# A state-space layer and a gated feed-forward net in one kernel: ScalarE's long stretches cut into parts with slots of their own

## The chip, the cores and the metric

The kernel runs on one core of a Trainium2 chip, all in float32. The metric is the time on the device in microseconds (us), the median of several runs; lower is better. Two kernels are compared on one chip.

## The reference

Input x is 2 sequences of 1024 tokens with 512 channels. Cut to what matters:

```python
xn = x * rsqrt(mean(x * x) + 1e-6) * norm_w
xn = xn * sigmoid((xn @ select_proj_w.T + select_proj_b) * select_gate)
delta, B, C = split(xn @ x_proj_w.T, 128)                # 128 wide each
dt = softplus(delta @ dt_proj_w.T + dt_proj_b)           # 512 wide
h = exp(dt * A) * h + (dt * xn) * B                      # per token, h is 512 x 128
y = sum_n h * C
x = layernorm(x + (y + x * D_param) @ out_proj_w.T)
out = layernorm(x + (silu(x @ w_gate.T) * (x @ w_up.T)) @ w_down.T)   # hidden 2048
```

(The D_param term takes the layer's own input x.) Everything but the recurrence over the 1024 tokens is matrix products and elementwise work; the recurrence is serial.

## The kernel before, in words

**The recurrence.** The state sits as 128 partitions (n) by 2 x 512 columns. VectorE makes four instructions a step t: two products `m = a * h` (L686, one for each sequence, SBUF to PSUM) and two sums into the new `h` (L706 or L709). If another engine has multiplied the row `u_bc` by B beforehand, the sum is a plain add (L706); if not, it is a scalar_tensor_tensor (L709) that multiplies as well. GpSimd scales one row of four in most pairs of steps (`on_pool`, L593), ScalarE three more (`on_act`, L1000) in stretches called quiet and where the load that the table LOAD gives for the steps' stages is at most 5. The exponentials `a` come from TensorE products (L1200, called P below) and a ScalarE Exp of 128x2048 (L981, called E); P writes four PSUM banks with no second buffer, so P and E alternate. `a` is a ring of 4 blocks of 4 steps: E of a slot that is a multiple of 8 waits until VectorE has left the oldest block. TensorE also forms y (L1276, "y rows", two steps at a time, 8 matmuls), and `h` is a ring of 6: VectorE's sum of step t waits until y of step t-6 is formed. `u_bc` is a ring of 5, filled from DRAM (`u_scratch`) by SyncE's queue.

**The order.** A chunk is 128 steps of the recurrence and has 256 slots, two a step, about 1.26 us each. TensorE's, ScalarE's and GpSimd's programs are written in order of slot, each engine in order. E stands at slots 0, 4, 8, ..., P two slots earlier (2, 6, 10, ...), the y rows at 0, 4, 8, ..., each ahead of what the plan puts at the same slot. Around these, a planner (`timetable`) places the stages of two threads: one prepares the next chunk (`stages_before`: x_in, sq, ms, root, xn, sel, gate, mask, xs, xp, dtp, pre, soft, c1 to c4, ut, utc), one finishes the chunk before (`stages_behind`: xd, ya, yt, ymc, outp, ln1, vt, vtc, 16 x gu with act, 16 x down with dnc, back, ln2, and the weight loads, tile). A stage is a tuple (name, index, slots until the next one). Both threads write one PSUM bank, `work`: a stage that fills it may only be placed after the slot in which the last user is emptied, and a thread that comes too early is moved to that slot. The stages c1 to c4, gm and gp and a few more (PIECES) run on GpSimd, one group every 4 slots.

**The last chunk.** In chunk 7 the thread of x = 6 runs as ever, and from slot 132 a second one (x = LAST = 7) finishes the first half of chunk 7; the second half is finished behind the recurrence, on 5 banks. Weight tiles (512 KB each, L916, ScalarE's queue) of x = 7 turn in 3 places. The second half's tiles go into the ring `a` as it comes free: ScalarE issues 8 of them at the start of step 1017 (slot 242, ahead of what is planned there), 4 at step 1021 (slot 250) and the other places later. TensorE's last y rows stand behind everything that is planned in the chunk.

**Stages that matter here.** `layer_norm` (L855 to L871) is 6 activations, 2 reads of an accumulator and a table load, in one run on ScalarE. `soft` (softplus) is a table load and 6 activations; `sq` is a square of 128x1024 and four scalings of 128x256. The parts of the plan before that the change moves, as the planner's rule gives them for chunks 1 to 6 (a stroke marks the thread that finishes):

```
6 sq0 | 11 ymc0' | 12 ms | 16 root | 17 20 outp' | 24 ln10' | 25 yt1' | 28 ymc1' | 29 32 sel 36 gate0 |
37 40 sel 44 gate1 | 45 48 outp' | 52 ln11' | 54 vt0' | 59 vt1' | 63 68 73 xp | 78 dtp0 82 soft0 |
82 to 181 gu', act' | 136 dtp1 140 soft1 | 184 to 232 down' | 206 ut0 209 utc0 210 ut1 213 utc1 |
236 back0' 240 ln20' 242 back1' 246 ln21'
```

Chunk 7: 121 to 157 down' of x = 6 with yt0' of x = 7 at 148; 160 163 outp', 166 ln10', 167 back0', 170 ln20', 171 vt0', 175 back1', 178 ln21', 179 to 226 gu' and act', 227 to 245 down', 247 back0', 250 ln20'. The tiles of the last downs are loaded at 231, 234, 236 and 239 (tiles 20 to 23).

Of the kernel before, what the change touches and what calls it, by code (L numbers as in the profile page):

```python
# [6 lines left out]
P = 128  # L7
# [9 lines left out]
GP = P // G  # L17
# [19 lines left out]
LOAD = {"sq": 24, "root": 16, "gate": 8, "mask": 5, "xpc": 2, "pre": 6, "soft": 40, "utc": 4, "ymc": 4, "ln1": 36, "vtc": 4,  # L37
        "act": 10, "dnc": 2, "ln2": 36}
# [35 lines left out]
def stages_before():  # L74

    yield from [("x_in", 0, 6), ("sq", 0, 4), ("ms", 0, 4), ("root", 0, 4)]
    for j in range(2):
        yield "xn", j, 0
    for j in range(2):
        yield from [("sel", 2 * j, 3), ("sel", 2 * j + 1, 4), ("gate", j, 1)]  # L80
    yield "mask", 0, 1
    yield "mask", 1, 3
    for j in range(2):
        yield "xs", j, 0
    for m in range(3):
        yield from [("xp", m, 4), ("xpc", m, 1)]
    for j in range(2):
        yield from [("dtp", j, 3), ("pre", j, 1), ("soft", j, 7), ("c1", j, 0), ("c2", j, 0), ("c3", j, 0), ("c4", j, 0)]
    for b in range(BATCH):
        yield from [("ut", b, 3), ("utc", b, 1)]  # L90
# [12 lines left out]
def stages_behind(x):  # L103

    both, ws, wide = x < LAST, halves(x), int(x < LAST - 1)
    ahead = W_RING if both else (TILES_14 if x == LAST else HB)
    if x <= LAST:
        for j in range(ahead):
            yield "tile", j, 0
    for w in ws:  # L110
        yield from [("xd", w, 0), ("ya", w, 0)] if w == ws[0] else [("xd*", w, 0), ("ya*", w, 0)]
    for w in ws:
        yield from [("yt", w, 2 + wide), ("ymc", w, 2)]
        if x == UNITS - 1:
# [12 lines left out]
    yield "rest", 0, 2 * wide  # L127
    for m in range(KB):
        for q in range(4):
            yield "down", 4 * m + q, (2 + q % 2 * wide if both else 1)  # L130
            if q % 2 and HB + ahead + 2 * m + q // 2 < TILES:
                yield "tile", HB + ahead + 2 * m + q // 2, 0
        yield "dnc", m, 1
    for w in ws:
        yield from [("back", w, 3 + wide), ("ln2", w, 1 + wide)]


def timetable(c):
# [6 lines left out]
    if c < LAST:  # L145
        threads.append([0, c + 1, list(stages_before())])
    if c == LAST:
        threads.append([2 * SLOTS * GP + 4, LAST, list(stages_behind(LAST))])
    if c > 0:
        x = c - 1 if c < CHUNKS else LAST + 1  # L150
        threads.append([0, x, list(stages_behind(x))])
    emptied, taken = 0, {}
    while threads:
        thread = min(threads, key=lambda t: t[0])
        slot, x, stages = thread
# [3 lines left out]
        if first and slot < emptied:  # L159
            thread[0] = emptied  # L160
            continue
# [25 lines left out]
def build(nc, xT, x_rows, vecs, d_row, sel_wT, xproj_wT, dt_wT, out_wT, A_log, gu_w, down_w, out_rows):  # L187
# [5 lines left out]
    with ctx:  # L193
# [46 lines left out]
        stat = sb("stat", [P, 8])  # L240
# [67 lines left out]
        def window_of(x, w):  # L308
# [33 lines left out]
        s_xd, s_ya, s_yt, s_outp, s_ln, s_vt, s_gu, s_th, s_sg, s_gm, s_gated, s_down, s_back = (  # L342
            sem(s) for s in ("s_xd", "s_ya", "s_yt", "s_outp", "s_ln", "s_vt", "s_gu", "s_th", "s_sg", "s_gm",
# [374 lines left out]
        def scalar(e):  # L718
# [3 lines left out]
            def before(x, stage, j):  # L722
# [6 lines left out]
                elif stage == "sq":  # L729
# [4 lines left out]
                    e.activation(T[:, :, :], U[:, :, :], ACT.Square).then_inc(s_sq, 1)  # L734
                    e.wait_ge(s_sq, x + 1)
# [36 lines left out]
                elif stage == "soft":  # L772
                    n = 5 * (2 * (x - 1) + j)
                    log_table()
                    e.wait_ge(s_work, emptied("dtp", x, j))
                    e.wait_ge(s_c2, 2 * x + j)
                    if j == 0:
                        e.wait_ge(d_us, 16 * BATCH * x)
                    e.activation(t_exp, pre[:, :, :], ACT.Abs).then_inc(s_soft, 1)
                    e.wait_ge(s_soft, n + 1)  # L780
                    e.activation(pre[:, :, :], pre[:, :, :], ACT.Relu).then_inc(s_relu, 1)
                    e.activation(t_exp, t_exp, ACT.Exp, scale=-1.0).then_inc(s_soft, 1)
                    e.wait_ge(s_soft, n + 2)
                    if j == 0:
                        e.wait_ge(s_xs, 2 * (x + 1))
                    e.activation(T[:, both, :], t_exp, ACT.Ln, bias=one[:, :]).then_inc(s_soft, 1)
                    e.activation(t_one, t_exp, ACT.Identity, bias=one[:, :]).then_inc(s_soft, 1)
                    e.wait_ge(s_soft, n + 4)
                    e.activation(t_one, t_one, ACT.Identity, bias=minus_one[:, :]).then_inc(s_soft, 1)
# [104 lines left out]
            def behind(x, stage, j):  # L894
# [29 lines left out]
                elif stage == "ln1":  # L924
# [3 lines left out]
                    layer_norm(bank("outp", x, j), emptied("outp", x, j), x, j, norms[stage, x, j])  # L928
# [25 lines left out]
                elif stage == "ln2":  # L954
                    e.wait_ge(s_back, window_of(x, j) + 1)
                    layer_norm(bank("back", x, j), emptied("back", x, j), x, j, norms[stage, x, j])
                    e.wait_ge(s_ln, 6 * (norms[stage, x, j] + 1))
# [67 lines left out]
            for slot in sorted(plans[CHUNKS]):  # L1025
                for stage, x, j in plans[CHUNKS][slot]:
                    if stage in ("ln1", "ln2"):
                        root_behind(stage, x, j)
                    elif stage not in ("ymc", "vtc"):
# [3 lines left out]
        def tensor(e):  # L1033
# [52 lines left out]
            def behind(x, stage, j):  # L1086
# [42 lines left out]
                elif stage == "vt":  # L1129
                    dst = bank(stage, x, j) if x > LAST else take(stage, x, j)  # L1130
                    if x <= LAST:
                        e.wait_ge(s_ln, 6 * (norms["ln1", x, j] + 1))
# [214 lines left out]
```

## Time and profile before

| what | value |
|---|---|
| median of 3 runs | 2693.13 us (2690.42 to 2694.03) |
| profiled execution, its own time | 2687.74 us |
| its span in the profile | 2685.9 us |
| VectorE busy | 2584.4 us (96%) |
| TensorE busy | 2316.6 us (86%) |
| ScalarE busy | 1708.6 us (64%) |
| GpSimd busy | 1028.3 us (38%) |
| recurrence, first product to last sum | 38.4 to 2620.5 us |
| behind it | 65.4 us |

Busy is the union of an engine's instructions. Idle time ahead of an instruction is given with the event that ended it. On this core an idle engine costs nothing unless the one that ends the chain waits for it, so the table alone doesn't say what a faster engine is worth.

### The profile page before, as it was taken

To read this page: it belongs to the slowest core of one execution; us is meant where nothing else is said; L and a number is where in the kernel's file an instruction comes from. 1 tells how busy PE (TensorE), PEld (TensorE's weight loads), DVE (VectorE), ACT (ScalarE), POOL (GpSimd) and SP (SyncE) were. 2 spreads that over 40 slices of the span, in tenths; PEclk is the share of its full clock that TensorE was granted. 3 is DMA by queue.
4 is the path that set the end of the run, shared out by engine and by line. 5 is a ranking of instruction groups with operands and counts; after the bars stand their busy time and mean duration, and the time that the engine had idled before them with its cause. 6 is when DMAs were issued, how large, how long until landed. Compare 5 with 4: busy or idle time off the path is not lost.

```text
span 2685.9 us, 48350 instructions
## 1 busy us (share of the span) xinstructions
PE 2316.6 (86%) x17036; PEld 1290.5 (48%) x17036; DVE 2584.4 (96%) x4160; ACT 1708.6 (64%) x2229; POOL 1028.3 (38%) x1031
## 2 busy tenths in 40 slices
PE   7866678998789987899779997799977998899998
PEld 4322224554345543555345553455534554465567
DVE  6999999999999999999999999999999999999892
ACT  5687766667566665667656666566666667654643
POOL 2343333443434434344333443344333443344320
PEclk8999999999999989999889998899989999999899
DMA  4566665777667876678757786577866777788694
GB/s 171 197 213 227 228 236 211 281 277 270 237 223 277 284 266 223 238 275 292 254 195 247 279 290 243 201 267 277 278 241 209 279 279 271 239 289 308 228 357 151
DMA packets 192060, 672.16 MB, mean 250 GB/s; under 512 B 20944, under 2 KB 26064, under 8 KB 191824
## 3 DMA queue, kind: packets, MB, share of 16 engines
q1 hardware_dynamic: 152432, 544.02, 57.5%
q10 hardware_dynamic: 39392, 125.06, 13.3%
q8 instruction: 140, 2.29, 0.3%
q14 instruction: 96, 0.79, 0.1%
HBM read 660.61 MB, written 8.39 MB: 249 GB/s over the span
## 4 chain that ended last, share of the span: by engine, by line
PE 39%; DVE 28%; ACT 15%; issue 12%; DMA 6%; POOL 0%; ACTq 0%; DVEq 0%; POOLq 0%
DVE h L709 14%; PE banks L1200 11%; DVE banks L686 10%; PE banks L1036 10%; PE banks L1176 7%; PE banks L1276 7%; ACT a L981 6%; DVE h L706 4%; DMA u_bc<-u_scratch 4%; ACT L720 2%; DMA U<-in_xT 1%; PE banks L1128 1%; PE banks L1124 1%; ACT u_bc L1000 1%; ACT v L862 1%
## 5 line engine op out<-in xcount | busy, mean ns | idle before, releaser
L981 ACT ACTIVATE a<-banks 128x2048 f32<-128x2048 f32 x512 | 960.7, 1876 | 604.3 <-PE banks L1200 563.1
L686 DVE TENSOR_TENSOR banks<-a,h 128x512 f32<-128x512 f32 x2048 | 1324.1, 688 | 4.1 <-ACT a L981 4.1
L709 DVE SCALAR_TENSOR_TENSOR h<-u_bc,BCt,banks 128x512 f32<-128x512 f32 x1482 | 1038.2, 732 | 5.4 <-PE banks L1276 5.4
L581 POOL TENSOR_TENSOR dexp<-spread,dt 128x512 f32<-128x512 f32 x512 | 539.1, 1053 | 821.2 <-DVE banks L686 779.2
L1200 PE MATMUL banks<-dexp,A 32*128 32x256 f32 x8192 | 623.6, 421 | 150.6 <-ACT a L981 149.0
L1276 PE MATMUL banks<-h,cz 128*32 128x512 f32 x4096 | 667.9, 623 | 94.4 <-DVE h L706 64.7
L1200 PEld LDWEIGHTS banks<-dexp,A 32*128 32x128 f32 x8192 | 390.3, 195 | 484.4 <-ACT a L981 347.7
L1036 PE MATMUL banks<-vT,w_ring 128*128 128x256 f32 x1792 | 449.9, 394 | 7.6 <-ACT up L948 6.9
L1036 PEld LDWEIGHTS banks<-vT,w_ring 128*128 128x128 f32 x1792 | 323.8, 190 | 175.4 <-issue 118.2
L706 DVE TENSOR_TENSOR h<-u_bc,banks 128x512 f32<-128x512 f32 x566 | 367.5, 673 | 19.9 <-PE banks L1276 19.9
L593 POOL TENSOR_SCALAR u_bc<-u_bc,BCt 128x512 f32<-128x512 f32 x266 | 184.1, 692 | 404.6 <-DVE banks L686 394.3
L1276 PEld LDWEIGHTS banks<-h,cz 128*32 128x32 f32 x4096 | 102.4, 109 | 351.4 <-issue 342.1
L1000 ACT ACTIVATE u_bc<-u_bc,BCt 128x512 f32<-128x512 f32 x300 | 203.6, 713 | 66.8 <-DMA u_bc<-u_scratch 65.4
L1176 PE MATMUL banks<-gated,w_ring 128*128 128x256 f32 x896 | 224.3, 393 | 10.2 <-ACT vT L953 7.7
L1176 PEld LDWEIGHTS banks<-gated,w_ring 128*128 128x128 f32 x896 | 161.3, 190 | 95.0 <-issue 60.1
L946 ACT ACTIVATE sg<-banks 128x256 f32<-128x256 f32 (+1 forms) x144 | 51.9, 361 | 180.5 <-PE banks L1036 179.1
L1036 PE MATMUL banks<-U,w_sel 128*128 128x256 f32 x256 | 78.0, 460 | 42.0 <-ACT gated L923 20.8
L525 POOL TENSOR_TENSOR gated<-gated,up 128x512 f32<-128x512 f32 x56 | 71.5, 1278 | 82.5 <-DVE banks L686 81.0
L522 POOL TENSOR_TENSOR gated<-gated,sg 128x512 f32<-128x512 f32 x56 | 71.5, 1278 | 81.8 <-DVE banks L686 81.8
L1036 PEld LDWEIGHTS banks<-U,w_sel 128*128 128x128 f32 x256 | 55.2, 225 | 74.5 <-ACT dt L748 26.3
L720 ACT ACT_TABLE_LOAD x55 | 70.6, 1283 | 4.5 <-issue 2.3
L950 ACT ACTIVATE sg<-sg,half 128x256 f32<-128x256 f32 (+1 forms) x144 | 71.4, 496 | 0.0
(177 smaller groups left out, 1284.9 us busy)
## 6 DMA issues: line engine op xcount, KB each, us to landing
u_bc<-u_scratch SPq DMA_DIRECT2D x1021, 512.0 KB, 4.6
w_ring<-in_gu_w ACTq DMA_DIRECT2D x112, 512.0 KB, 5.5
w_ring<-in_down_w ACTq DMA_DIRECT2D x56, 512.0 KB, 5.7
a<-in_gu_w ACTq DMA_DIRECT2D x16, 512.0 KB, 12.7
a<-in_down_w ACTq DMA_DIRECT2D x8, 512.0 KB, 4.4
x_tok<-in_x_rows SPq DMA_DIRECT2D x15, 256.0 KB, 5.7
out_rows<-v ACTq DMA_DIRECT2D x15, 256.0 KB, 3.4
U<-in_xT ACTq DMA_DIRECT2D x7, 512.0 KB, 6.0
```

Source lines behind the costliest of these rows:

```text
L581: e.tensor_tensor(dexp[:, q % E_RING, :, :, :], spread[:, :].unsqueeze(1).unsqueeze(1).to_broadcast(shape), by_step[:, :, first:first + BS ...
L593: e.tensor_scalar(part, part, BCt[c % 2][:, 0, tl:tl + 1], 1.0, ALU.mult, ALU.mult).then_inc(s_zp, 1)
L686: e.tensor_tensor(m_ps[:, b, :], a[:, blk % A_RING, b, s, :], h[:, (t - 1) % H_RING, b * D:(b + 1) * D], ALU.mult).then_inc(s_m, 1)
L706: e.tensor_tensor(h[:, t % H_RING, part], u_bc[:, t % U_RING, part], m_ps[:, b, :], ALU.add).then_inc(s_h, 1)
L709: e.scalar_tensor_tensor(h[:, t % H_RING, part], u_bc[:, t % U_RING, part], BCt[c % 2][:, 0, b * TB + tl:b * TB + tl + 1], m_ps[:, b, :], ...
L720: e.preload_act_table_set("natural_log_exp_and_others")
L981: e.activation(dst.rearrange("p b t (x j) -> p x (b t) j", j=GP), src.rearrange("p g (i r j) -> p (g i) r j", i=PAIR, j=GP), ACT.Exp, scal ...
L1000: e.activation(part, part, ACT.Copy, scale=BCt[c % 2][:, 0, b * TB + tl:b * TB + tl + 1]).then_inc(s_za, 1)
L1036: last = e.matmul(dst, w, x, start=i == 0, stop=i == len(pairs) - 1)
L1176: last = e.matmul(dst, tile[:, sub * (HB // 4) + i, :], hidden(x, hb), start=hb == 0, stop=hb == HB - 1)
L1200: last = e.matmul(dst[:, g, i * COLS:(i + 1) * COLS], A[rows, q % 2 * PAIR + i, :], lays, start=True, stop=True)
L1276: last = e.matmul(y_ps[group * GP:(group + 1) * GP, :], cz[:, first:first + GP], h[:, t % H_RING, b * D:(b + 1) * D], start=i == 0, stop=i ...
```

## The change

Every long stretch of ScalarE is split into stages that the planner places apart:

- `layer_norm` becomes `center` (stages ln1, ln2: mean, subtract, square sum) and `normalize` (ln1b, ln2b: table load, rsqrt by Ln and Exp, scale). The statistics get two sets, the semaphore s_ln becomes two.
- `soft` becomes three parts (indices 3j, 3j+1, 3j+2): Abs and Relu; table load, Exp and Ln; two Identity passes.
- `sq` becomes two: the square, and the four scalings.
- LOAD gets new figures for the parts; some gaps between stages change.
- A thread that was moved back for the bank gets a fourth field, the slot to which it was last moved. Of two threads at one slot, the one with the smaller field goes first; before it was the first in the list.

The instructions themselves, their shapes and their number stay as they are, apart from which rows ScalarE scales.

```diff
-LOAD = {"sq": 24, ..., "soft": 40, ..., "ln1": 36, ..., "ln2": 36}
+LOAD = {"sq": 12, ..., "soft": 14, ..., "ln1": 24, "ln1b": 16, ..., "ln2": 24, "ln2b": 16}
...
-    yield from [("x_in", 0, 6), ("sq", 0, 4), ("ms", 0, 4), ("root", 0, 4)]
+    yield from [("x_in", 0, 6), ("sq", 0, 2), ("sq", 1, 2), ("ms", 0, 4), ("root", 0, 4)]
...
-        yield from [("dtp", j, 3), ("pre", j, 1), ("soft", j, 7), ("c1", j, 0), ...]
+        yield from [("dtp", j, 3), ("pre", j, 2), ("soft", 3 * j, 2), ("soft", 3 * j + 1, 3), ("soft", 3 * j + 2, 2), ("c1", j, 0), ...]
...
-        yield from [("outp", 2 * w, 3), ("outp", 2 * w + 1, 3 + wide), ("ln1", w, 2 * w if both else 4)]
+        yield from [("outp", 2 * w, 3), ("outp", 2 * w + 1, 3 + wide), ("ln1", w, 2 if both else 1), ("ln1b", w, 2 * w if both else 1)]
...
-        yield from [("back", w, 3 + wide), ("ln2", w, 1 + wide)]
+        yield from [("back", w, 3 + wide if x < LAST else 2), ("ln2", w, 1 + wide if x < LAST else 0), ("ln2b", w, 0)]
...
-        thread = min(threads, key=lambda t: t[0])
+        thread = min(threads, key=lambda t: (t[0], t[3]))
...
         if first and slot < emptied:
             thread[0] = emptied
+            thread[3] = emptied
             continue
...
-                    e.activation(T[:, :, :], U[:, :, :], ACT.Square).then_inc(s_sq, 1)
-                    e.wait_ge(s_sq, x + 1)
+                    e.activation(T[:, :, :], U[:, :, :], ACT.Square).then_inc(s_sq, 1)
+                elif stage == "sq":
+                    e.wait_ge(s_sq, x + 1)
                     for k in range(KB):
...
+            def center(src, turn, x, w, n):
+                rows, st = v(x, w), stat[:, n % 2, :]
...
+                e.activation(squares(x), rows, ACT.Square, accum_out=st[:, 2:3]).then_inc(s_ln_a, 1)
+            def normalize(x, w, n):
+                rows, st = v(x, w), stat[:, n % 2, :]
                 log_table()
...
+                e.activation(rows, rows, ACT.Copy, scale=st[:, 4:5]).then_inc(s_ln_b, 1)
```

## Rows read from the trace of the kernel before

**Rows 1.** The page's busy times: share of the span, instructions of each engine.
```profile
PE 2316.6 (86%) x17036; PEld 1290.5 (48%) x17036; DVE 2584.4 (96%) x4160; ACT 1708.6 (64%) x2229; POOL 1028.3 (38%) x1031
```

**Rows 2.** Waits of VectorE at 400:2300, then 2300:2620 (total, times, longest us).
```profile
DVE h L706 <- PE banks L1276: 12.7, 8, 4.0
...
DVE h L706 <- PE banks L1276: 7.2, 5, 4.6
DVE h L709 <- PE banks L1276: 1.8, 1, 1.8
```

**Rows 3.** The page's costliest groups: count | busy us, mean ns | idle before.
```profile
L709 DVE SCALAR_TENSOR_TENSOR h<-u_bc,BCt,banks 128x512 f32<-128x512 f32 x1482 | 1038.2, 732 | 5.4 <-PE banks L1276 5.4
...
L706 DVE TENSOR_TENSOR h<-u_bc,banks 128x512 f32<-128x512 f32 x566 | 367.5, 673 | 19.9 <-PE banks L1276 19.9
...
L1000 ACT ACTIVATE u_bc<-u_bc,BCt 128x512 f32<-128x512 f32 x300 | 203.6, 713 | 66.8 <-DMA u_bc<-u_scratch 65.4
```

**Rows 4.** VectorE's timeline at four waits: start, us, instruction [idle before].
```profile
1083.46 0.69 DVE L706 TENSOR_TENSOR h<-u_bc,banks 128x512 f32<-128x512 f32 x1 [1.01 <-PE banks L1276]
...
1382.04 0.69 DVE L706 TENSOR_TENSOR h<-u_bc,banks 128x512 f32<-128x512 f32 x1 [3.97 <-PE banks L1276]
...
1409.38 0.69 DVE L706 TENSOR_TENSOR h<-u_bc,banks 128x512 f32<-128x512 f32 x1 [2.22 <-PE banks L1276]
...
2524.98 0.69 DVE L706 TENSOR_TENSOR h<-u_bc,banks 128x512 f32<-128x512 f32 x1 [4.59 <-PE banks L1276]
```

**Rows 5.** TensorE's timeline in chunk 3, 1034:1086.
```profile
1036.31 3.50 PE L1036 MATMUL banks<-U,w_sel 128*128 128x256 f32 x8 [3.47 <-ACT gated L923]
...
1049.22 3.41 PE L1036 MATMUL banks<-U,w_sel 128*128 128x256 f32 x8 [3.33 <-ACT dt L748]
...
1060.83 1.98 PE L1128 MATMUL banks<-w_out,gated 128*128 128x512 f32 x4 [1.91 <-ACT dt L748]
...
1077.41 2.09 PE L1200 MATMUL banks<-dexp,A 32*128 32x256 f32 x16 [3.45 <-ACT a L981]
1079.43 2.08 PE L1140 MATMUL banks<-ident,v 128*128 128x128 f32 x8
1081.43 1.94 PE L1276 MATMUL banks<-h,cz 128*32 128x512 f32 x8
```

**Rows 6.** ScalarE's timeline in chunk 3, same stretch.
```profile
1033.92 1.86 ACT L981 ACTIVATE a<-banks 128x2048 f32<-128x2048 f32 x1
...
1040.96 1.88 ACT L981 ACTIVATE a<-banks 128x2048 f32<-128x2048 f32 x1 [4.70 <-PE banks L1200]
...
1070.57 0.59 ACT L858 ACTIVATE v<-banks 128x512 f32<-128x512 f32 x1
...
1075.50 1.86 ACT L981 ACTIVATE a<-banks 128x2048 f32<-128x2048 f32 x1
```

**Rows 7.** ScalarE's last write of u_scratch in chunk 2, and landing of both writes.
```profile
944.91 0.33 ACTq L796 DMA_DIRECT2D u_scratch<-t_both  x1
...
DMA to landing us min/median/max: 4.4/4.9/5.4
```

**Rows 8.** ScalarE's timeline at the end of chunk 7: the last tile, then eight.
```profile
2601.79 0.34 ACTq L916 DMA_DIRECT2D t_both<-in_down_w  x1
...
2605.48 5.27 ACTq L916 DMA_DIRECT2D a<-in_gu_w  x8
```

**Rows 9.** Landing of the first (issued 2605.5) and the eighth (2610.2) of them.
```profile
DMA to landing us min/median/max: 8.1/8.1/8.1
...
DMA to landing us min/median/max: 13.7/13.7/13.7
```

**Rows 10.** TensorE's timeline at the end of chunk 7.
```profile
2608.78 2.05 PE L1176 MATMUL banks<-w_sel,t_both 128*128 128x128 f32 x16
2611.29 1.10 PE L1184 MATMUL banks<-U,ident 128*128 128x512 f32 x2 [0.46 <-ACT w_xp L953]
...
2620.66 1.92 PE L1276 MATMUL banks<-h,cz 128*32 128x512 f32 x4 [1.47 <-DVE h L709]
```

More of the change, by code:

```diff
@@ L35 @@
 SLOTS = 2
-LOAD = {"sq": 24, "root": 16, "gate": 8, "mask": 5, "xpc": 2, "pre": 6, "soft": 40, "utc": 4, "ymc": 4, "ln1": 36, "vtc": 4,
-        "act": 10, "dnc": 2, "ln2": 36}
+LOAD = {"sq": 12, "root": 16, "gate": 8, "mask": 5, "xpc": 2, "pre": 6, "soft": 14, "utc": 4, "ymc": 4, "ln1": 24, "ln1b": 16, "vtc": 4,
+        "act": 10, "dnc": 2, "ln2": 24, "ln2b": 16}
 LIGHT = 5
@@ L87, in stages_before @@
     for j in range(2):
-        yield from [("dtp", j, 3), ("pre", j, 1), ("soft", j, 7), ("c1", j, 0), ("c2", j, 0), ("c3", j, 0), ("c4", j, 0)]
+        yield from [("dtp", j, 3), ("pre", j, 2), ("soft", 3 * j, 2), ("soft", 3 * j + 1, 3), ("soft", 3 * j + 2, 2), ("c1", j, 0), ("c2", j, 0), ("c3", j, 0), ("c4", j, 0)]
     for b in range(BATCH):
@@ L145, in timetable @@
     if c < LAST:
[L146 removed]
+        threads.append([0, c + 1, list(stages_before()), 0])
     if c == LAST:
[L148 removed]
+        threads.append([2 * SLOTS * GP + 4, LAST, list(stages_behind(LAST)), 0])
     if c > 0:
         x = c - 1 if c < CHUNKS else LAST + 1
[L151 removed]
+        threads.append([0, x, list(stages_behind(x)), 0])
     emptied, taken = 0, {}
     while threads:
[L154 to L155 removed]
+        thread = min(threads, key=lambda t: (t[0], t[3]))
+        slot, x, stages, _ = thread
         stage, j, gap = stages[0]
@@ L239, in build @@
         v_all = sb("v", [P, 2, D])
-        stat = sb("stat", [P, 8])
+        stat = sb("stat", [P, 2, 5])
         moments = sb("moments", [P, 12])
@@ L728, in before @@
                                 ).then_inc(d_x, 16)
-                elif stage == "sq":
+                elif stage == "sq" and j == 0:
                     e.wait_ge(d_x, 16 * (x + 2))
@@ L782, in before @@
[L782 to L789, printed above, removed]
+                    half_d, part = j // 3, j % 3
@@ L927, in behind @@
                         e.wait_ge(s_dt, 2 * CHUNKS)
-                    layer_norm(bank("outp", x, j), emptied("outp", x, j), x, j, norms[stage, x, j])
+                    center(bank("outp", x, j), emptied("outp", x, j), x, j, norms["ln1", x, j])
+                elif stage == "ln1b":
+                    normalize(x, j, norms["ln1", x, j])
                 elif stage == "vtc":
@@ L955, in behind @@
                     e.wait_ge(s_back, window_of(x, j) + 1)
-                    layer_norm(bank("back", x, j), emptied("back", x, j), x, j, norms[stage, x, j])
-                    e.wait_ge(s_ln, 6 * (norms[stage, x, j] + 1))
+                    center(bank("back", x, j), emptied("back", x, j), x, j, norms["ln2", x, j])
+                elif stage == "ln2b":
+                    normalize(x, j, norms["ln2", x, j])
+                    e.wait_ge(s_ln_b, 3 * (norms["ln2", x, j] + 1))
                     e.dma_start(out_rows[window_of(x, j)], v(x, j)).then_inc(d_out[j], 16)
@@ L1028, in scalar @@
                         root_behind(stage, x, j)
-                    elif stage not in ("ymc", "vtc"):
+                    elif stage not in ("ymc", "vtc", "ln1b", "ln2b"):
                         behind(x, stage, j)
@@ L1131, in behind @@
                     if x <= LAST:
-                        e.wait_ge(s_ln, 6 * (norms["ln1", x, j] + 1))
+                        e.wait_ge(s_ln_b, 3 * (norms["ln1", x, j] + 1))
                     for k in range(KB):
```

59 lines of the change are left out of this document (34 added, 25 removed).

## The prediction

> **What bounds the kernel.** I read the page's busy times first: VectorE is busy 96% of the span, ScalarE 64% [rows 1]. The recurrence holds VectorE from 38.4 to 2620.5, so what counts is (a) how long its instructions are, (b) its waits in there, (c) the 65.4 us behind it. The waits of VectorE, asked by stretch, are short and have one cause: y rows that come too late for the ring of `h`; 12.7 us in 8 waits up to 2300, 9.0 us in 6 waits after it [rows 2]. So at most 21.7 us can be had from a smoother ScalarE. The timeline says where they lie: at step 35 of chunks 3 and 4, at step 25 of chunk 4, and 4.59 us in chunk 7 [rows 4].
>
> TensorE's rows say why y is late. It is in order, and stands behind ScalarE: 3.47 us for ymc1', 3.33 and 1.91 for gate0 and gate1, 3.45 for E [rows 5]. Meanwhile P and the y rows queue behind the stage that waits. The last is the layer norm: ln11' runs from 1070.57 to E at 1075.50, 4.9 us in which E can't start [rows 6]; vt1' (2.08 us) then goes ahead of the y rows at slot 60, which start at 1081.43, and VectorE waits until 1083.46 [rows 4, 5].
>
> **The plan after.** I followed the planner's rule through the diff's lists. Chunks 1 to 6: sq0 6, sq1 8, ln10' 24, ln1b0' 26, yt1' 26, ymc1' 29, sel 30 33 38 41, gate 37 45, outp' 46 49, ln11' 53, ln1b1' 55, vt0' 57, xp 61 66 71, dtp0 76, vt1' 80, soft 81 83 86, gu' from 85 to 177, dtp1 181 (136 before: the thread that was moved back last now loses every tie to the gu's), soft 186 188 191, down' 185 to 225, back0' 229, ln20' 233, ut0 234, ln2b0' 235, utc0 237, utc1 241, ln21' 246, ln2b1' 248. Chunk 7: down' of x = 6 from 124 to 157, back' 160 164, ln20' 163, ln2b0' 164, ln21' 167, ln2b1' 168, only then x = 7: yt0' 168, ln10' 178, gu' 185 to 230, down' 233 to 251, back0' 253, ln20' 255. Tiles 20 to 23: 237, 240, 242, 245.
>
> **Part 1, scalings: +2.7.** With the new LOAD and places, ScalarE scales 255 rows instead of 300; GpSimd's 266 stay. 45 sums go from L706 (673 ns) to L709 (732 ns): 45 x 0.059 = 2.7 us, all on VectorE, nothing hides it [rows 3]. The planner's rule gives 300 and 266 for the kernel before as the trace has them, so this term is sure to some tenths.
>
> **Part 2, chunks 1 to 6: -12.** The parts of ln1 fall between the same two E's (24 and 28, 52 and 56), so the split itself moves no E there. What moves is the one-slot shift. P stands at slots 2, 6, 10, ..., ahead of a stage at the same slot. Before, sel0 (29) was ahead of P30, sel2 (37) ahead of P38, outp' (45) ahead of P46; after, they are at 30, 38, 46 and behind it. In chunk 3: P30 needs only E28 (1033.92 + 1.86 = 1035.8) and takes about 1.1, so E32 can start at 1037.0 instead of 1040.96 [rows 6]: 4.0 us. P38 and P46 then run inside the waits for gate0 and gate1 [rows 5]: 1.1 each. With vt1' gone from slot 59 to 80, the y rows of slot 60 gain another 2.1. Together about 8.3 us at step 30, 5.1 at step 25. The waits there add up to 3.97 + 2.22 + 0.2 in chunk 4, the worst, and 1.0 in chunk 3 [rows 4]: all smaller. From there on E follows VectorE (ring `a`), no further gain is possible. I take 12.0 of the 12.7. Bounds: 0 and -12.7; a cost too is possible if the queue before slot 60 isn't what I think, at most the 12.7 again.
>
> The work that was moved: vt1' at 80, soft0 and gu' close by load ScalarE for 10 slots (12.6 us) with about 14.4 us; y is then 2 us later there, under the 11 us that the ring gives. Downs in 40 slots instead of 48 fill TensorE, as the gu's do now: nothing, by the same 11 us. The wait that is added: utc1 goes from 213 to 241, the u_scratch write behind it lands 5.4 us after its issue [rows 7], about slot 249; SyncE's queue holds the next chunk's first `u_bc` load (from slot 248) until then, and GpSimd's scaling and VectorE's sum of step 0 wait for it. I count some 25 us of ScalarE's work into the 34 us from 229 to 256, so utc1 is 4 to 5 us late and the load ready some 4 us ahead of need: nothing. If that cover were gone: 1 to 3 us for each of 6 chunks.
>
> **Part 3, chunk 7 up to slot 185: -3.** Here the parts do straddle an E (164, 168). Before, three whole layer norms lie within 12 slots, 4.9 us each, and the 4.59 us wait is theirs [rows 4, 6]. After, two lie within 160 to 170 and ln10' at 178: ScalarE is over-full by 4 us instead of 7. Against it: gu' and downs of x = 6 start 3 slots later and end at the same slot; yt0' has left, so TensorE is 3.8 - 1.1 = 2.7 us further behind at slot 157, just where VectorE already waits. Of 9.0 us I keep 6. Bounds: -9 and +7 (the 2.7 and the 4.6 both on top).
>
> **Part 4, the end: +10.** Before, the last tile (23) is issued at 2601.79 and the eight loads of 512 KB into `a` at 2605.48 [rows 8]. These landed 8.1 us after issue for the first (2613.6) and 13.7 for the eighth (2623.9) [rows 9]: 1.3 to 1.5 us each, one after the other. After, tile 22 (slot 242) and tile 23 (245) stand behind the eight (start of step 1017, slot 242). The eight still land by about 2621 to 2624, so tile 22 at 2622.6 to 2625.2 and tile 23 1.3 later. TensorE reaches down12 by about 2614 and waits. Then four downs (2.05 for two [rows 10], up to twice that at the half clock after a stop), y rows 1.0, back0' 2.1, the last y rows 1.0: y is complete at 2631 to 2636 instead of 2620.66 + 1.92 = 2622.6 [rows 10]. What follows hangs on y and shifts whole. +8.5 to +13.5; some of the products behind now find the clock high: I take +10. Queued behind: ln20' and 4 more loads on ScalarE, ready about when the tail's first Ln is wanted; 0 to +1. Bounds of the term: 0 (if the tiles don't queue) and +15.
>
> By the Trainium skill (DMA: Bandwidth & Descriptors, Queues, rings and completion order) an engine consumes descriptors in ring order, but "completion is **not FIFO per issuing engine**". Taken as leave for the two tiles to overtake, part 4 is nothing and the sum lower by 10. This trace's landings are in order [rows 9], which says nothing of a tile put behind.
>
> **Part 5, the rest: 0.** Same instructions and table loads; splitting sq brings E8 ahead of four scalings, but chunk by chunk ring `a` holds E16.
>
> **Sum.** 2687.7 (the profiled execution) + 2.7 - 12 - 3 + 10 = 2685.4. The median of the runs is 5.4 above that execution. The three runs differ by 3.6 among themselves, and the only loose thing I see in the trace is how late y comes; in part 2 I expect that looseness to go. I add 1.6 and forecast **2687.0**.
>
> **Rivals.**
> R1, *the splits split nothing* (slower): ln1's parts stay between the same E's, and if the late y rows hang on the 4.9 us of ScalarE's work and not on the order of P and stage, part 2 is 0: 2687.7 + 2.7 - 3 + 10 = 2697.4 from the profiled execution, 2702.8 from the median; centre 2700. For: the 3.45 us wait for E at 1077.41 [rows 5] remains word for word. Against: it would still have to reach the ring's 11 us. It decides from 9 us of 12.7 that stay.
> R2, *the tiles aren't held up*: part 4 is 0, 2677. For: the queue feeds many engines. Against: landings one by one [rows 9].
> R3, *chunk 7 gets worse*: part 3 is +4 instead of -3, 2694. For: TensorE further behind at 157.
> R4, *starved thread*: utc1 late, 6 x 2 us, 2699. Against: 4 us of cover.
>
> **Chances.** Forecast (2681 to 2692) 0.50, R1 0.17, R2 0.12, R3 0.14, R4 0.07. A run here can't tell less than about 0.2% (5.4 us) from nothing. Faster (under 2687.7) takes 0.30 of the forecast's 0.50, R2's 0.12 and 0.03 of R3 and R1: 0.45. Within 0.2% (to 2698.5): 0.20 of the forecast, 0.10 of R3, 0.05 of R1: 0.35. Slower, the rest of R1 and R3 and R4: 0.20. Range with 8 in 10: 2675 to 2701.
>
> **What the profile after would show.** L1000 x255, L706 x521, L709 x1527. VectorE's waits for y rows before 2300 near 0 (over 6 us: part 2 wrong). In each chunk P ahead of sel0, sel2, outp'. In chunk 7 waits of 3 to 9 us near steps 75 to 90. At the end TensorE idle for about 8 to 12 us for a tile of `in_down_w`, and the last y rows 8 to 14 us behind VectorE's last sum instead of 2. No wait of VectorE or GpSimd for `u_bc` at a chunk's start. The prediction is wrong if that idle time is missing, or if y is late in a new place.

## The result, and the profile after

The changed kernel takes 2734.23 us (median of 4 runs, 2722.27 to 2738.97), the kernel before 2691.78 us (4 runs, 2683.30 to 2694.03): ratio 1.0157, 95% interval 1.0116 to 1.0198. It is slower by 1.6%. The forecast was 2687.0 with a range of 2675 to 2701: wrong, and by more than any rival allowed for. The experiments were run on three chips; the time that is given for the kernel before beside each is that of the same chip, and ratios are to be compared rather than times.

The profiled executions were 2687.74 us before and 2731.46 us after, spans 2685.9 and 2729.7. The page after, busy times and the groups that answer to [rows 1, 3] (the group's last part is the idle time ahead of it):

```profile
PE 2308.2 (85%) x17036; PEld 1295.4 (47%) x17036; DVE 2606.9 (96%) x4160; ACT 1669.3 (61%) x2178; POOL 1028.5 (38%) x1031
...
L687 DVE TENSOR_TENSOR banks<-a,h 128x512 f32<-128x512 f32 x2048 | 1346.2, 700 | 3.4 <-ACT a L997 3.4
L710 DVE SCALAR_TENSOR_TENSOR h<-u_bc,BCt,banks 128x512 f32<-128x512 f32 x1527 | 1073.4, 735 | 2.6 <-PE banks L1292 2.6
...
L707 DVE TENSOR_TENSOR h<-u_bc,banks 128x512 f32<-128x512 f32 x521 | 341.6, 676 | 32.2 <-ACT u_bc L1016 16.3
...
L1016 ACT ACTIVATE u_bc<-u_bc,BCt 128x512 f32<-128x512 f32 x255 | 170.8, 713 | 32.8 <-DMA u_bc<-u_scratch 32.7
```

The counts of part 1 are right: 521 plain sums, 1527 that multiply, 255 scalings. But the plain sums now wait 32.2 us instead of 19.9 (all sums 34.8 instead of 25.3), half of it for a releaser that wasn't in the list before: a row scaled by ScalarE. And VectorE is busy 22.5 us longer, of which the new mix of sums explains 2.7. VectorE's waits by stretch, 400:2350 and then 2350:2652 (total, times, longest), which answer to [rows 2]:

```profile
DVE h L707 <- ACT u_bc L1016: 16.3, 6, 3.2
DVE h L707 <- PE banks L1292: 3.9, 3, 1.3
...
DVE h L707 <- PE banks L1292: 9.3, 5, 4.0
DVE h L707 <- POOL u_bc L594: 2.4, 1, 2.4
DVE h L710 <- PE banks L1292: 0.2, 1, 0.2
```

The busy time hides a second loss. VectorE's timeline and its neighbours' in chunk 2 (start, us, instruction; "x2" are two in a row):

```profile
883.92 0.40 ACT L962 ACTIVATE up<-banks 128x256 f32<-128x256 f32 x1
883.93 1.39 DVE L710 SCALAR_TENSOR_TENSOR h<-u_bc,BCt,banks 128x512 f32<-128x512 f32 x2
884.19 0.53 ACT L964 ACTIVATE sg<-sg,half 128x256 f32<-128x256 f32 x1
...
884.86 1.27 POOL L523 TENSOR_TENSOR gated<-gated,sg 128x512 f32<-128x512 f32 x1 [2.17 <-ACT sg L964]
885.25 2.03 DVE L687 TENSOR_TENSOR banks<-a,h 128x512 f32<-128x512 f32 x2
```

Two products take 2.03 us instead of the usual 1.28 to 1.30: the first lasts until 0.56 us after the end of GpSimd's gm (884.86 + 1.27 = 886.13). In the trace before, each of the 56 gm's started 1.36 or 1.37 us after its step began, beside the two sums; after, that is still the median, but 20 of the 56 start only 1.9 to 2.14 us after it, and the next product runs into them. I call a product long that lasts over 0.06 us more than the median one, and count what it lasts beyond the median: over chunks 1 to 7 that adds up to 5.4 us before and 24.5 after (7.2 and 25.9 with chunk 0; 15.4 of the 25.9 in 24 products that start while a gm runs, the rest beside other GpSimd work). So the later end of the loop, 30.5 us (2620.5 to 2651.0), is: waits +8.8, long products +18.7, part 1's +2.7, rest 0.3 (the loop also starts 1.0 us earlier). Behind the loop stand another 13.2 us (65.4 to 78.6).

Where it lies by chunk, in us, chunks 0 to 7, from last sum to last sum in the two traces (chunk 0 from its first sum, so 127 steps):

```
before  316.1  319.2  319.8  320.4  325.9  323.0  320.3  334.8
after   314.6  324.6  328.0  327.8  327.7  324.5  324.3  339.5
```

In chunks 2 to 4 the long products stand at steps 76, 82, 88, 94 and 100 (steps counted from 0 here; the prediction's and the expectations' step numbers for the waits are one higher), and the wait for a scaled row at step 100: the stretch in which the thread that finishes runs gu' and act', and the 10 steps behind it. TensorE's waits there, chunk 3 of after (1133:1253):

```profile
PE banks L1052 <- ACT up L962: 11.0, 6, 1.8
PE banks L1092 <- ACT up L962: 1.8, 1, 1.8
PE banks L1192 <- ACT pre L771: 1.7, 1, 1.7
```

Before, in the same steps (1122:1238), there was one such wait:

```profile
PE banks L1036 <- ACT up L948: 1.1, 1, 1.1
```

The timeline of one of them, ScalarE, TensorE and GpSimd of after:

```profile
1193.58 1.88 ACT L997 ACTIVATE a<-banks 128x2048 f32<-128x2048 f32 x1 [4.04 <-PE banks L1216]
...
1195.88 0.40 ACT L962 ACTIVATE up<-banks 128x256 f32<-128x256 f32 x1
1196.15 0.53 ACT L964 ACTIVATE sg<-sg,half 128x256 f32<-128x256 f32 x1
1196.34 1.99 PE L1052 MATMUL banks<-vT,w_ring 128*128 128x256 f32 x8 [1.83 <-ACT up L962]
...
1196.82 1.27 POOL L523 TENSOR_TENSOR gated<-gated,sg 128x512 f32<-128x512 f32 x1 [1.72 <-ACT sg L964]
```

The act' that empties the `work` bank (its three reads end with `up`) sits behind an E of 1.88 us, although ScalarE had been idle for 4.04 us before that E. The next gu' waits 1.83 us for the bank; sg, and with it gm, is late by the E.

### The profile page after: what moved, and what is told of

Its sections match the earlier page's. It is cut to its first block, busy times and chain, and to the rows that moved or that the text cites. A ratio compares the mean times of both kernels' runs of the same rounds, so it can differ in the third digit from the quotient of the medians.

```text
span 2729.7 us, 48254 instructions
## 1 busy us (share of the span) xinstructions
PE 2308.2 (85%) x17036; PEld 1295.4 (47%) x17036; DVE 2606.9 (96%) x4160; ACT 1669.3 (61%) x2178; POOL 1028.5 (38%) x1031
## 4 chain that ended last, share of the span: by engine, by line
PE 52%; DVE 22%; issue 12%; ACT 10%; DMA 3%; ACTq 0%; DVEq 0%
PE banks L1052 20%; PE banks L1216 13%; DVE h L710 9%; PE banks L1292 8%; DVE banks L687 8%; PE banks L1192 7%; DVE h L707 5%; ACT a L997 4%; DMA u_bc<-u_scratch 2%; ACT L721 1%; ACT sg L960 1%; ACT u_bc L1016 1%; PE banks L1092 1%; PE banks L1144 1%; ACT gated L961 1%
## 5 line engine op out<-in xcount | busy, mean ns | idle before, releaser
L687 DVE TENSOR_TENSOR banks<-a,h 128x512 f32<-128x512 f32 x2048 | 1346.2, 700 | 3.4 <-ACT a L997 3.4
L710 DVE SCALAR_TENSOR_TENSOR h<-u_bc,BCt,banks 128x512 f32<-128x512 f32 x1527 | 1073.4, 735 | 2.6 <-PE banks L1292 2.6
L1216 PE MATMUL banks<-dexp,A 32*128 32x256 f32 x8192 | 616.5, 417 | 154.2 <-ACT a L997 153.3
L1292 PE MATMUL banks<-h,cz 128*32 128x512 f32 x4096 | 646.2, 626 | 83.0 <-DVE h L707 58.4
L1052 PE MATMUL banks<-vT,w_ring 128*128 128x256 f32 x1792 | 458.9, 400 | 88.3 <-ACT up L962 79.8
L707 DVE TENSOR_TENSOR h<-u_bc,banks 128x512 f32<-128x512 f32 x521 | 341.6, 676 | 32.2 <-ACT u_bc L1016 16.3
L1292 PEld LDWEIGHTS banks<-h,cz 128*32 128x32 f32 x4096 | 96.6, 109 | 320.5 <-issue 309.8
L1016 ACT ACTIVATE u_bc<-u_bc,BCt 128x512 f32<-128x512 f32 x255 | 170.8, 713 | 32.8 <-DMA u_bc<-u_scratch 32.7
```

The costliest lines, as they stand in the source:

```text
L687: e.tensor_tensor(m_ps[:, b, :], a[:, blk % A_RING, b, s, :], h[:, (t - 1) % H_RING, b * D:(b + 1) * D], ALU.mult).then_inc(s_m, 1)
L707: e.tensor_tensor(h[:, t % H_RING, part], u_bc[:, t % U_RING, part], m_ps[:, b, :], ALU.add).then_inc(s_h, 1)
L710: e.scalar_tensor_tensor(h[:, t % H_RING, part], u_bc[:, t % U_RING, part], BCt[c % 2][:, 0, b * TB + tl:b * TB + tl + 1], m_ps[:, b, :], ...
L1016: e.activation(part, part, ACT.Copy, scale=BCt[c % 2][:, 0, b * TB + tl:b * TB + tl + 1]).then_inc(s_za, 1)
L1052: last = e.matmul(dst, w, x, start=i == 0, stop=i == len(pairs) - 1)
L1216: last = e.matmul(dst[:, g, i * COLS:(i + 1) * COLS], A[rows, q % 2 * PAIR + i, :], lays, start=True, stop=True)
```

## The experiments

Around gu' two things differ from before in chunks 1 to 6. The planner now puts act' at 90, 96, 102, ... instead of 87, 93, 99, ...: every second one falls on a multiple of 4, where E stands, and at a shared slot E is written first. And dtp1 with its softplus, which used to break up the row of gu's at 136, comes at 181, since it loses every tie. Each experiment takes these or another part by itself.

**e1, the turns alone, without any split** (the kernel before with the new tie rule; act' stays at odd slots).

```diff
-        thread = min(threads, key=lambda t: t[0])
+        thread = min(threads, key=lambda t: (t[0], t[3]))
...
+            thread[3] = emptied
```

> The kernel before with the new rule for ties alone, no long stretch split. ScalarE scales 300 rows as before, the gu stages of chunks 1 to 6 keep their slots (act at odd slots), dtp1 and the second softplus move from slot 136 to 178, and in chunk 7 tiles 22 and 23 come behind the eight loads into a. Theory (act directly behind an Exp when its slot is a multiple of 4, which makes gm late and into VectorE's next product, and rows scaled late): no products longer than 0.8 us in chunks 1 to 6, no wait for a scaled row; only the end costs, VectorE's wait for the last y rows 12 to 15 us: 2700 to 2710. Rival (the crowding that the tie rule makes behind the gu stages is the cause): long products or waits at steps 99 to 101 here too, 2715 to 2735.

Measured: 2693.99 us beside 2688.05 for the kernel before on that chip; ratio 1.0021 (1.0007 to 1.0036). Chunks 1 to 6 wait 4.8 us for y (12.7 before), the long products stay at 6.3, and behind the loop it is 75.8. The time is below the 2700 to 2710 that I had set down. The tie rule costs little by itself, and what it costs is at the end.

**e2, the splits alone** (the changed kernel with the old tie rule up to chunk 6; chunk 7 keeps the new one, since its plan depends on it).

```diff
-        thread = min(threads, key=lambda t: (t[0], t[3]))
+        thread = min(threads, key=lambda t: (t[0], t[3] if c == LAST else 0))
```

> The changed kernel with the old rule for ties in chunks 1 to 6 (chunk 7 keeps the new one). dtp1 goes back from slot 181 to 115 and the first acts stay on even slots. Theory (slot of act): the long products stay, about as many (15 to 19 us over the six chunks, perhaps at other steps), 2720 to 2740. Rival (the tie rule's crowding): long products and the waits at steps 99 to 101 go, 2695 to 2710.

Measured: 2697.98, ratio 1.0040 (1.0025 to 1.0055). act' stands at even slots, half of them on an E, and TensorE waits for it nearly as much as in the changed kernel, 12.4 us in the stretch 1120:1236 (13.2 there). But the row of gu's has pauses again, dtp1 at slot 115 and ut and utc at 179 to 186, and VectorE sees little of it: waits 4.7 in chunks 1 to 6, long products 8.9. The time is in the rival's range, not in that of the theory of act's slots: even slots without the other half don't make the 1.6%, and e1 shows the same of the other half.

**e3, the changed kernel, gu' one slot later** (all splits, the new tie rule, act' at odd slots).

```diff
-    ("vtc", w, 2)
+    ("vtc", w, 3 if wide and w else 2)
```

> The changed kernel with one number more: the gap behind the second vtc in chunks 1 to 6 is 3 instead of 2, so that all gu and act stages lie one slot later, act at odd slots; ScalarE scales 237 rows instead of 255 (1.1 us more for VectorE). Theory (slot of act): TensorE's waits for act in the gu phase fall from 11 to 13 us a chunk to under 3, products longer than 0.8 us are gone from chunks 1 to 6 (15 to 19 us less), the waits at steps 99 to 101 go from 20 us to under 6: 2695 to 2708. Rival (the tie rule or the splits themselves): no change, 2725 to 2740.

Measured: 2692.27, ratio 1.0012 (0.9996 to 1.0029). One slot of delay, and 38 of the 42.5 us are gone (by the differences from the kernel before on each chip): VectorE doesn't wait at all from 400 to 2315, long products 6.7.

**e4, gm and gp one group later in the changed kernel**, to take GpSimd's product off VectorE's without touching ScalarE.

```diff
+            group += stage in ("gm", "gp") and x < LAST and j < HB // 2 - 1
             while taken.get(group, 0)
```

> The changed kernel with gm and gp of chunks 1 to 7 (but for the last pair) one group of 4 slots later on GpSimd; act stays on even slots and TensorE as late as in the changed kernel. Theory (a gm that waits for act starts late in the step and VectorE's next product is held until it ends): the products longer than 1.2 us go, 12 to 18 us of VectorE's time, while its waits for scaled rows and y at steps 99 to 101 stay or grow as the chain behind them is the same: 2712 to 2724. Rival (the long products come from something else, DMA traffic or ScalarE): they stay, 2725 to 2740.

Measured: 2731.47, ratio 1.0176 (1.0150 to 1.0202): no gain, a miss. The long products fell from 24.5 to 12.4, but the waits of chunks 1 to 6 stayed (21.3), and this profile, at 2719.7 of span, is the quickest of its 4 runs. It was run again below.

**e5, e3 with the loads into `a` put later.** Eight of them go out at step 1020 in place of 1017, so that the last two tiles are ahead of them in ScalarE's queue.

```diff
-USED_UP = {SEQ - 7: (0, 1), SEQ - 3: (2,)}
+USED_UP = {SEQ - 4: (0, 1), SEQ - 3: (2,)}
```

> The changed kernel with gu and act one slot later in chunks 1 to 6, and ScalarE issues the eight loads into a at step 1020 (slot 248) instead of 1017, behind tiles 22 and 23. Theory (tiles 22 and 23 queue behind the eight): VectorE's wait for the last y rows falls from 14 us to 1 to 3, the stretch behind the loop from 79.2 to 66 to 69 us; 2692 - 11 = 2679 to 2683, faster than before by about 0.2 to 0.3%. Rival (the end is late because TensorE has too much to do in the last 20 slots): the wait falls by less than 5 us, 2687 to 2691.

Measured: 2683.75 (12 runs) beside 2687.96, ratio 0.9984 (0.9974 to 0.9994). Behind the loop 71.3 us instead of 79.2: this is what the order in the queue costs, with the place at which ScalarE issues the loads. The wait for the last y fell to 6.97 us, not to the 1 to 3 expected. What is left of it stands in the timelines of ScalarE, and of VectorE's last y:

```profile
2605.61 7.50 ACTq L928 DMA_DIRECT2D a<-in_gu_w  x12
2613.17 0.28 ACT L967 ACTIVATE w_xp<-banks 128x128 f32<-128x128 f32 x1 [7.28 <-issue]
...
2618.35 0.75 DVE L514 TENSOR_TENSOR v<-v,banks 128x256 f32<-128x256 f32 x2 [6.97 <-PE banks L1292]
```

Twelve load instructions take ScalarE 7.50 us, and the copy that back0' wants stands behind them.

**e6, no splits, but act' at even slots** (e1 with dtp0 given three more slots, which moves gu' from 82 to 85).

```diff
-        yield from [("dtp", j, 3), ...
+        yield from [("dtp", j, 6 - 3 * j), ...
```

> The kernel before with the new rule for ties and a gap of 6 instead of 3 behind dtp0, which puts gu from 85 on and act at 90, 96, 102, ..., the very slots of the changed kernel; no stretch is split. ScalarE scales 282 rows instead of 300 (1.1 us). Theory (slots of act, with nothing to break the row of gu stages): long products and waits as in the changed kernel, 25 to 40 us over the kernel with the tie rule alone (2694): 2720 to 2735. Rival (the splits are what costs): 2694 to 2700.

Measured: 2776.16, ratio 1.0328 (1.0295 to 1.0362), above what I had set down. Chunks 1 to 6 take 330 to 339 us each, long products of chunks 1 to 7 34.4. Its waits of VectorE (400:2400) and of TensorE (1133:1253):

```profile
DVE h L707 <- ACT u_bc L1001: 30.3, 18, 4.1
DVE h L707 <- PE banks L1277: 19.9, 9, 3.8
DVE h L710 <- PE banks L1277: 3.3, 4, 1.3
...
PE banks L1037 <- ACT up L949: 14.0, 8, 1.8
PE banks L1037 <- ACT pre L770: 1.7, 1, 1.7
```

The loss needs no split: e1 and this kernel differ by three slots (and 18 scaled rows, 1.1 us), and by 82 us. With even slots and the new ties the kernel without splits takes 2776, with them 2734 to 2739: there the splits, with the slots that move with them, are worth some 40 us. At odd slots they are worth 1.7 (e1 2693.99, e3 2692.27), which is nothing.

**e7, ScalarE scales no rows in chunks 1 to 7** (126 go, which stood at steps 88 to 111 of chunks 1 to 6, and the 129 of chunk 0 stay; VectorE multiplies itself), to see whether the wait for scaled rows is a cause.

```diff
-            return t < TB or t < LAST * TB and 88 <= t % TB < 112
+            return t < TB
```

> The changed kernel, in which ScalarE scales rows in chunk 0 alone (quiet is false elsewhere); VectorE multiplies those rows itself. The waits for scaled rows at steps 99 to 101 (16 to 20 us) can't be; the sums get longer by 129 x 0.06 = 7.7 us. Theory (ScalarE's lateness in the gu phase is the cause, and the waits for rows only its first sign): y comes just as late, long products stay at 15 to 20 us; time 2720 to 2732. Rival (the scaled rows themselves hold ScalarE and so make it late): the long products go too, 2705 to 2712.

Measured: 2745.93, ratio 1.0211 (1.0188 to 1.0235), above the expectation; the changed kernel's ratios are 1.0157 and 1.0179 (e11), and 126 sums that multiply are 7.4 us. The releaser changes, the time doesn't go. VectorE's waits, 400:2370:

```profile
DVE h L707 <- PE banks L1292: 20.0, 15, 2.8
DVE h L710 <- PE banks L1292: 0.4, 1, 0.4
```

The wait for scaled rows was the place where the lateness of ScalarE and TensorE showed first; without it y shows it.

**e8, e5 with more rows on ScalarE** (324 in place of e5's 237, by a higher limit of load).

```diff
-LIGHT = 5
+LIGHT = 14
```

> As e5_phase_tail, and LIGHT is 14 instead of 5, so that ScalarE scales 324 rows instead of 237: 87 x 0.06 = 5.2 us less for VectorE, if ScalarE has the time beside an act or a part of softplus. Theory (in the new phase ScalarE has slack there): 2675 to 2678. Rival (it makes act late again): waits for scaled rows or long products, over 2683.

Measured: 2681.60 (12 runs) beside 2687.96, ratio 0.9971 (0.9958 to 0.9985). 590 plain sums, no waits in chunks 1 to 6, chunk by chunk 319.5 to 319.6 us. The expected 2675 to 2678 wasn't reached, but with e10 this is the quickest version, 0.3% below the kernel before.

**e9, the plan of the changed kernel untouched, act' written ahead of E at a shared slot in ScalarE's program.**

```diff
+                    for stage, x, j in now:
+                        if stage == "act":
+                            behind(x, stage, j)
                     if SLOTS * t + i in EXP_AT:
                         exponents(EXP_AT[SLOTS * t + i], p_ps)
...
+                    for stage, x, j in now:
+                        if stage != "act":
+                            behind(x, stage, j)
+                            before(x, stage, j)
```

> The changed kernel with its plan untouched; in ScalarE's program alone, an act whose slot is also that of an Exp (8 of 16 in each of the chunks 1 to 6, 8 of 32 in chunk 7) goes ahead of the Exp. Theory (an act directly behind a 1.88 us Exp holds the one bank and so TensorE, and makes gm late): TensorE's waits for act in the gu phase fall from 12.8 us a chunk to under 3, no long products from gm, no waits at steps 99 to 101: 2695 to 2708, what the one-slot shift gave. Rival (the shift helped because it moved other stages too): at most a third of the 40 us, over 2720.

Measured: 2692.17 (10 runs) beside 2686.76, ratio 1.0013 (0.9998 to 1.0028): the time of e3, from another place. The changed kernel takes 2739.12 on this chip (e11). TensorE's waits at 1120:1236, then VectorE's at 2320:2612 (from 400 to 2320 the view is empty):

```profile
PE banks L1297 <- DVE h L710: 0.9, 1, 0.9
PE banks L1197 <- ACT pre L771: 0.2, 1, 0.2
...
DVE h L707 <- PE banks L1297: 10.5, 5, 5.4
```

Nothing in the plan, the splits or the turns has changed here; only which of two ScalarE stages at one slot goes first. So the loss in the loop comes from an act' that stands behind an E. What e2 adds is that it costs that much only in a row without a pause: dtp1 is at 181 here too, and without the waits the unbroken row costs nothing.

**e10, e8 with e9's order, and the loads into `a` split otherwise**: four at step 1020, eight at step 1023, the last.

```diff
-USED_UP = {SEQ - 4: (0, 1), SEQ - 3: (2,)}
+USED_UP = {SEQ - 4: (0,), SEQ - 1: (1, 2)}
```

> As e8_scale (gu one slot later, LIGHT 14), with act ahead of Exp at a shared slot (only chunk 7 has such slots) and the loads into a spread: 4 at step 1020, 8 at step 1023, so that ScalarE's last dnc isn't behind twelve issues. Theory: VectorE's wait for the last y rows 7 us down to 3 to 5, and chunk 7's waits for y down by 1 to 4 us: 2674 to 2680. Rival (chunk 7 is late because TensorE and the layer norms are over-full, not because of act): only the 2 to 4 us of the end, 2677 to 2681.

Measured: 2681.73 (12 runs) beside 2686.76, ratio 0.9974 (0.9963 to 0.9986), just outside the rival's range. Behind the loop it is 69.5 (71.1 in e8), VectorE waits 3.38 us for the last y instead of 6.7, but the time is that of e8: what follows takes half of it back.

**e11, the changed kernel again**, unchanged, and **e12, e4 again** beside it.

> The changed kernel as it is, beside e12 on one chip: 2722 to 2739 as in its first runs, long products 20 to 26 us, waits 28 to 36 us in chunks 1 to 7.

> e4_gm_late once more, in more runs and beside the changed kernel. If the held products cost time of their own: 8 to 12 us under e11. If the chain behind ScalarE sets the time anyway and VectorE only waits instead: within 3 us of it.

Measured: 2739.12 (ratio 1.0179, 1.0155 to 1.0204) and 2741.39 (1.0185, 1.0154 to 1.0215). The product's group and VectorE's waits in 400:2350, e11 and then e12:

```profile
L687 DVE TENSOR_TENSOR banks<-a,h 128x512 f32<-128x512 f32 x2048 | 1344.0, 697 | 3.2 <-ACT a L997 3.2
...
DVE h L707 <- ACT u_bc L1016: 16.2, 6, 3.2
DVE h L707 <- PE banks L1292: 3.9, 3, 1.3
```

```profile
L688 DVE TENSOR_TENSOR banks<-a,h 128x512 f32<-128x512 f32 x2048 | 1333.5, 692 | 4.1 <-ACT a L998 4.1
...
DVE h L708 <- ACT u_bc L1017: 19.1, 6, 3.2
DVE h L708 <- PE banks L1293: 16.7, 6, 3.0
```

With gm moved, the products are shorter by 10.5 us over the program (long ones 14.7 instead of 25.3 in chunks 1 to 7), and the time is no shorter. The waits of chunks 1 to 6 are 36.0 us here, 20.3 in e11 and 21.3 in e4, which is the kernel of e12: most of that difference isn't gm's. In all four profiles of these two kernels, chunks 2 to 6 take one of two times, and only chunks of like time can be compared (per chunk, us):

| chunks 2 to 6 | take | waits | long products |
|---|---|---|---|
| changed kernel (first profile and e11), 5 and 6 | 324.3 to 324.5 | 1.9 to 2.0 | 2.6 to 3.0 |
| gm late, e4, 2 to 6 | 324.2 to 324.4 | 3.2 | 1.3 to 1.5 |
| changed kernel, 2 to 4 | 327.7 to 328.0 | 4.5 | 3.4 to 3.8 |
| gm late, e12, 2 to 6 | 327.7 | 6.1 | 1.8 |

What the products lose, the waits gain, at either time. So the long products are real time of VectorE but not a cause of their own: a product that is held keeps VectorE back by as much as it would otherwise wait for TensorE and ScalarE, which run late anyway. The 3.3 us between the two times go with TensorE's clock: in each of the chunks at 327.7 two groups of gu matmuls that follow a wait for act' run slowly (in over 2.3 us instead of 1.99), in each of those at 324.4 one. The changed kernel's runs go the same way: 2722.27 us at a granted clock of 0.957, 2737.0 and 2738.97 at 0.948 and 0.947.

## Why the prediction was wrong

The moved row of gu' and act' was given no price, and it is this row that costs what the loop lost; the rest of the sum came out within some 8 us a term.

**Part 1, +2.7: right.** The counts are those foretold.

**Part 2, the waits of before (-12): the size right, the reason in part.** None of the waits of [rows 2, 4] in chunks 1 to 6 is left: before step 98 VectorE doesn't wait there. With the gu' row mended (e3, e9) its waits in these chunks are 0, the whole 12.7. R1 (the splits split nothing) falls as it was put, and P does stand ahead of sel0 now (chunk 3, 1047.00 and 1049.02). But e1 has neither splits nor that shift and only 4.8 of the 12.7 is left: chunks 4 and 5, which waited 6.4 and 3.7 us, wait 1.0 and 1.1. So at most 4.8 is the shift's by these runs. Whether the other 7.9 goes by the new ties or differs from run to run was not tried; that they add up to my 12 is in part luck.

**Part 2, "The work that was moved": the step that failed.** I had both facts in the list of the plan (gu' from 85 instead of 82, dtp1 at 181 instead of 136) and gave them no price: "Downs in 40 slots instead of 48 fill TensorE, as the gu's do now: nothing, by the same 11 us." I costed ScalarE's load in the first 10 slots and didn't lay act' on the grid of the E's. I took the row as filling TensorE without a wait, but it comes to stand with every second act' on a slot of an E and behind it. What the runs show in place of "nothing":

1. TensorE waits for the bank, mostly 1.83 us each time, 12.8 us in the stretch of chunk 3 above where it was 1.1, and over the program 90.8 us in 55 waits instead of 6.9 in 7. e9, which changes this order alone, has 2.2 us in 6.
2. The clock adds to it. After one of these waits 8 matmuls take 3.61 us instead of 1.99, and the granted clock of that stretch (1178.8:1182.6) is 0.55, the lower level of 1.2 GHz for most of it. This is so behind 10 of the 55 waits (13.6 us more in all; behind 2 of the 7 before); behind the others the 8 matmuls take 1.99 us or less, although the wait is mostly as long:

```profile
1178.90 3.61 PE L1052 MATMUL banks<-vT,w_ring 128*128 128x256 f32 x8 [1.83 <-ACT up L962]
```

3. With dtp1 gone to 181 the row has no break in which TensorE could catch up. e2, with dtp1 at 115 and ut and utc at 179, has nearly the same waits of TensorE (85.1 us in 49) and VectorE waits only 4.7 us. That the slack of the ring (the 11 us of the prediction, an estimate) is used up before an unbroken row ends fits this, but no run moved a pause alone with act' at even slots.
4. ScalarE, behind in turn, scales its rows late. ScalarE and VectorE at step 100 of chunk 3:

```profile
1266.81 1.94 ACT L1016 ACTIVATE u_bc<-u_bc,BCt 128x512 f32<-128x512 f32 x3
...
1267.63 0.69 DVE L707 TENSOR_TENSOR h<-u_bc,banks 128x512 f32<-128x512 f32 x1 [3.18 <-ACT u_bc L1016]
```

5. gm starts late and holds a product. The gm rows, before and after (first the form, then what ended the idle time ahead of all of gm's forms; 25.1 and 25.5 us in 8 of the waits for sg are VectorE's, behind the loop, which leaves GpSimd 12.2 us in 3 before and 66.0 in 28 after):

```profile
L522 POOL TENSOR_TENSOR gated<-gated,sg x56: 1269/1278/1286, 480.9 to 2444.9; 128x512 f32<-128x512 f32 x56
...
  DVE banks L686: 94.1, 61
  ACT sg L950: 37.3, 11
```

```profile
L523 POOL TENSOR_TENSOR gated<-gated,sg x56: 1263/1276/1842, 483.5 to 2473.7; 128x512 f32<-128x512 f32 x56
...
  ACT sg L964: 91.5, 36
  DVE banks L687: 60.0, 36
```

The price in chunks 1 to 6 is 20.4 us of waits and 18.4 us of long products, against the 12.7 us of waits that went.

**Part 3, -3 forecast, +4.7 measured: the gain isn't there.** Chunk 7 went from 334.8 to 339.5: waits from 9.0 to 11.9, long products from 4.6 to 6.1, the rest 0.3. That has the size of R3 (+4), but the second profile of the same kernel (e11) has 335.3 with waits of 7.7: +0.5. So the term lies between 0 and +5 by two profiles, and R3 isn't shown. With e9's order the chunk takes 336.0 and waits 10.5. That TensorE is further behind at slot 157 for want of yt0' there, my argument for R3, was not tried by itself.

**Part 4, +10 forecast, +13.2 measured (13.8 in e11): the mechanism is right, the size a little small.** The end of the chunk, ScalarE and then TensorE, which answer to [rows 8, 10]:

```profile
2636.98 5.37 ACTq L928 DMA_DIRECT2D a<-in_gu_w  x8
2642.39 0.46 ACTq L928 DMA_DIRECT2D dt<-in_down_w  x1
```

```profile
2655.71 3.75 PE L1192 MATMUL banks<-w_sel,dt 128*128 128x128 f32 x16 [4.84 <-DMA dt<-in_down_w]
2659.25 2.54 PE L1192 MATMUL banks<-w_sel,t_both 128*128 128x128 f32 x16
...
2664.67 1.06 PE L1292 MATMUL banks<-h,cz 128*32 128x512 f32 x8
```

Tile 22 landed at 2655.6, 13.2 us after its issue and 1.3 us behind the eighth of the loads: in order, so R2 is refuted. By the Trainium skill (DMA: Bandwidth & Descriptors, Queues, rings and completion order) completion need not follow the order of issue; in this trace, with all nine on one queue and each 512 KB, it did. I had TensorE idle for 8 to 12 us; it was idle for 4.84 there, since its own row reached the tile 6 us later than I took, and then ran the four downs in 6.1 us (2655.71 to 2661.79), within the "up to twice" of 4. The last y rows ended 14.7 us behind VectorE's last sum (2665.7 and 2651.0; 8 to 14 forecast). e5 gives the price of the order in the queue, 7.9 us. The rest, some 6 (71.3 in e5, 65.4 before), I had at "0 to +1". In e5 it is ScalarE's own issue time for the loads, 7.50 us for 12, in front of the copy for back0'; e10 splits them and comes to 69.5. The last 4 were not taken apart.

**R4 (starved thread): refuted.** VectorE and GpSimd don't wait for `u_bc` at a chunk's start.

**The sum.** Measured by its terms: part 1 +2.7; the old waits -12.7; the moved row +38.0 (waits 20.4, long products 18.4 less the 0.8 of before); chunk 7 +4.4 without its share of part 1 (waits 2.9, products 1.5); the end +13.2; and chunk 0, which I had at 0, -2.3 (waits 7.7 to 5.8, products 1.8 to 1.4). That is +43.3 of the 43.8 in the span, in this pair of profiles.

## What to carry to other kernels

When a hand-written plan shifts a row of stages by a few slots, lay the row on the grid of every periodic instruction that shares its engine, and ask at each shared slot which is written first: here one slot (ratio 1.0157 to 1.0012) or one order (2739 to 2692 us on one chip) was worth more than everything the splits were for. Cost a long row by what it loses at each turn times its length, and against the pause in which it could catch up (the part of the pause is argued from e2), not by the slack of one turn. And split a bulk load from a late small one in a queue by which of the two is awaited first.

## What the runs showed that I hadn't expected

A product of two SBUF operands on VectorE that starts while GpSimd runs a tensor_tensor is held until that one ends: in the trace after, 66 products start with over 0.2 us of such an instruction left; 61 of them end 0.55 to 0.56 us after it (two products took 2.03 us instead of 1.30), and in the other five it is GpSimd's instruction that lasts 0.5 to 1.1 us longer than its median. The sums, with one operand in PSUM, are not held: 705 of them start over 0.2 us before such an instruction ends, and the longest of these lasts 0.75 us. The Trainium skill (SBUF — State Buffer, section SBUF: two separate sides) has this as a rule, a lock held for the whole instruction between a VectorE instruction with two SBUF inputs and a GpSimd one that reads SBUF; the trace agrees (gm ends at 886.13; the products from 885.25 last 0.73 us too long). That it costs nothing extra while TensorE and ScalarE are the late ones is what the table under e12 shows.

The eight loads of 512 KB on one queue landed 1.2 to 1.3 us apart (2.2 between the first two), with the tile behind them one more such step later.
